# The next block's input is transposed by VectorE in place of TensorE, into a doubled place, in loops unrolled by two

## The reference

```python
xn = _layernorm(x, axis=-1)
x = x + _L0_attn_ref(xn, Wq, Wk, Wv, Wog, Wig, big, Wfg, bfg, gamma, Wout) + _L0_ffn_ref(xn, w_gate, w_up, w_down)

# attention: q, k, v, o_preact = xn @ W.T; i_pre, f_pre soft-capped at 15; 8 heads, DQ 32, DV 64
def step(carry, xs):
    C, n, m = carry
    q_t, k_t, v_t, i_t, f_t = xs
    f_log = jax.nn.log_sigmoid(f_t)
    m_new = jnp.maximum(f_log + m, i_t)
    F = jnp.exp(f_log + m - m_new)
    I = jnp.exp(i_t - m_new)
    C_new = F[..., None, None] * C + (I[..., None] * k_t)[..., :, None] * v_t[..., None, :]
    n_new = F[..., None] * n + I[..., None] * k_t
    ...
    h = h_num / denom[..., None]
...
h_norm = _multihead_norm(h, gamma).reshape(B, S, -1)
y = (jax.nn.sigmoid(o_preact) * h_norm) @ Wout.T

# ffn, 2048 hidden: gated = silu(x @ w_gate.T) * (x @ w_up.T); gated @ w_down.T
```

## Time and profile before

| | |
|---|---|
| median of 3 runs | 3141.33 us (3140.83 to 3141.61) |
| the profiled execution | 3142.2 us, with a span of 3140.4 us from the first to the last instruction |
| granted TensorE clock, mean | 0.995 |
| busy: PE, PE weight loads, DVE, ACT, POOL | 98%, 71%, 61%, 36%, 24% |

### The profile page before, as it was taken

The page is one execution under the profiler, slowest core; times in us unless marked ns, Lnnn a source line. Parts: engine busy times, 40 slices in busy tenths (PEclk is TensorE's granted clock), DMA queues, the critical chain, the costliest instruction groups (busy, mean ns, idle before and its releaser), DMA issues.

```text
span 3140.4 us, 61802 instructions
## 1 busy us (share of the span) xinstructions
PE 3077.6 (98%) x22450; PEld 2238.5 (71%) x22450; DVE 1914.3 (61%) x4380; ACT 1120.7 (36%) x2150; POOL 751.4 (24%) x1120
## 2 busy tenths in 40 slices
PE   3999999999999999999999999999999999999999
PEld 2677777777777777777777777777777777777776
DVE  8666656656556666556566566565566665665665
ACT  5333333333323333333333333333233333333332
POOL 4222222222222221222222222222222212222222
PEclk8999999999999999999999999999999999999999
DMA  5000000000000000000000000000000000000000
GB/s 222 8 14 13 13 7 7 13 13 13 13 0 13 13 13 13 7 7 13 13 13 13 7 7 13 13 13 13 0 13 13 13 13 7 7 13 13 13 13 7
DMA packets 20333, 51.08 MB, mean 16 GB/s; under 512 B 1506, under 2 KB 1634, under 8 KB 18274
## 3 DMA queue, kind: packets, MB, share of 16 engines
q1 hardware_dynamic: 20322, 50.95, 4.4%
HBM read 34.16 MB, written 16.78 MB: 16 GB/s over the span
## 4 chain that ended last, share of the span: by engine, by line
PE 97%; DVE 2%; issue 0%; DMA 0%; ACT 0%; SPq 0%; DVEq 0%; ACTq 0%
PE work L1082 21%; PE work L1084 21%; PE work L1083 21%; PE acc L1083 7%; PE acc L1084 7%; PE acc L1082 7%; PE o_bank L1189 3%; PE o_bank L1249 2%; PE work L1255 2%; PE s_bank L1236 1%; PE work L1267 1%; PE work L1261 1%; PE e_bank L1230 1%; PE work L1166 1%; DVE amax L732 1%; PE work L1221 1%
## 5 line engine op out<-in xcount | busy, mean ns | idle before, releaser
L1082 PE MATMUL work<-xt,weights 128*128 128x256 f16 x4608 | 1257.0, 273 | 0.1
L1084 PE MATMUL work<-xt,weights 128*128 128x256 f16 x4608 | 1256.8, 273 | 0.0
L1083 PE MATMUL work<-xt,weights 128*128 128x256 f16 x4608 | 1256.8, 273 | 0.0
L543 POOL TENSOR_TENSOR arena<-arena 128x256 f16<-128x256 f32 x512 | 348.6, 681 | 1715.4 <-ACT arena L670 1715.4
L955 DVE SCALAR_TENSOR_TENSOR arena<-arena,work 128x256 f32<-128x256 f32 x512 | 215.2, 420 | 537.9 <-ACT arena L666 534.8
L1082 PEld LDWEIGHTS work<-xt,weights 128*128 128x128 f16 x4608 | 478.8, 104 | 69.8 <-DVE arena L958 0.2
L1083 PEld LDWEIGHTS work<-xt,weights 128*128 128x128 f16 x4608 | 451.2, 98 | 69.9
L1084 PEld LDWEIGHTS work<-xt,weights 128*128 128x128 f16 x4608 | 451.1, 98 | 52.5
L666 ACT ACTIVATE arena<-work,unscale 128x256 f32<-128x256 f32 x512 | 241.2, 471 | 587.1 <-PE work L1084 586.7
L670 ACT ACTIVATE arena<-arena 128x256 f16<-128x256 f32 x512 | 213.4, 417 | 589.1 <-DVE arena L958 589.1
L1082 PE MATMUL acc<-weights,arena 128*128 128x512 f16 x1024 | 388.2, 379 | 0.0
(11 more groups left out here) (209 smaller groups left out, 4024.1 us busy)
## 6 DMA issues: line engine op xcount, KB each, us to landing
arena<-x_dram SPq DMA_DIRECT2D x33, 512.0 KB, 3.3
out_dram<-arena SPq DMA_DIRECT2D x32, 512.0 KB, 2.8
weights<-w_g_dram SPq DMA_DIRECT2D x4, 1024.0 KB, 13.4
weights<-w_u_dram SPq DMA_DIRECT2D x4, 1024.0 KB, 20.8
arena<-w_d_dram SPq DMA_DIRECT2D x4, 1024.0 KB, 26.3
arena<-w_qk_dram SPq DMA_DIRECT2D x1, 1024.0 KB, 6.5
arena<-w_v_dram SPq DMA_DIRECT2D x1, 1024.0 KB, 8.5
weights<-w_o_dram SPq DMA_DIRECT2D x1, 1024.0 KB, 15.9
```

Of the source, the lines that this page charges most:

```text
L543: g.tensor_tensor(hh[:, j % HB, 1, :], tt[:, j % 2, :], hh[:, j % HB, 0, :], ALU.subtract).then_inc(h_ready, 1)
L1082: t.matmul(dst, w[0], a[0], start=first, stop=False, skip_group_check=True)
L1083: t.matmul(dst, w[0], a[1], start=False, stop=False, skip_group_check=True)
L1084: return t.matmul(dst, w[1], a[0], start=False, stop=last, skip_group_check=True)
```

## The change

The order of the steps on all engines changes. mean_var goes behind tile 3, xn0 behind tile 4, xn1 behind tile 6. ScalarE now writes the normalized chunks into the places of `qs` and `kf`. A new step "turn c q" on VectorE transposes 32 tokens of chunk c: four VectorE transposes (of 32x32 blocks), each from the 32 partitions of quarter q to one of the four groups of 32 partitions, 32x128 fp32 elements each, into `xnt` in SBUF. Behind tile 5 stand turn00, turn01, turn02; behind tile 6 turn03; behind tile 7 turn10, turn11; behind tile 9 turn12, turn13. "xT0" (behind tile 7) and "xT1" (behind tile 11) are no longer on TensorE: they are only the high and the low half, now read from SBUF. `xt` has two places, used in turn, so every loop body is written for two blocks (`one_block` called twice in a loop of 16). xT0 and xT1 leave `USES`, which has 34 entries; att1 is put into bank 1. `gates` waits for the semaphore xt_ready. In the part ahead of the loop the places of the first input change, and GpSimd clears qq and kk after the first input was transposed.

The diff, cut to its core (left out: the names and the place of the new buffers, `xt` handed on as an argument, and the same loop of pairs on the other engines):

```diff
--- before.py
+++ after.py
@@ -54,18 +54,19 @@
 
 USES = (["gates", "q", "k", "v0", "v1", "ffn0", "ffn1", "ffn2", "ffn3", "wT", "ffn4", "wbc", "kT", "ffn5", "o0",
          "ffn6", "st0", "ffn7", "ffn8", "st1", "ffn9", "ffn10", "st2", "ffn11", "hoT0", "ffn12", "st3", "o1",
-         "ffn13", "att0", "ffn14", "ffn15", "hoT1", "xT0", "xT1", "att1"])
+         "ffn13", "att0", "ffn14", "ffn15", "hoT1", "att1"])
 NUSE = len(USES)
-assert NUSE % 3 == 0
+BANK = {name: n % 3 for n, name in enumerate(USES)}
+BANK["att1"] = 1
 
 
 def bank_no(name):
-    return USES.index(name) % 3
+    return BANK[name]
 
 
 def uses_of(b, before=NUSE):
 
-    return len(USES[b:before:3])
+    return len([name for name in USES[:before] if BANK[name] == b])
 
 
 
@@ -81,18 +82,20 @@
 AFTER[0] = ["stack0"]
 AFTER[1] = ["stack1"]
 AFTER[2] = ["stack2", "stats"]
-AFTER[3] = ["wT", "stack3"]
-AFTER[4] = ["wbc", "kT", "es0"]
-AFTER[5] = ["o0", "mean_var"]
-AFTER[6] = ["es1", "pv0", "xn0"]
+AFTER[3] = ["wT", "stack3", "mean_var"]
+AFTER[4] = ["wbc", "kT", "es0", "xn0"]
+AFTER[5] = ["o0", "turn00", "turn01", "turn02"]
+AFTER[6] = ["es1", "pv0", "turn03", "xn1"]
+AFTER[7] = ["turn10", "turn11", "xT0"]
 AFTER[8] = ["es2", "pv1", "center0"]
-AFTER[9] = ["scale0", "xn1"]
+AFTER[9] = ["scale0", "turn12", "turn13"]
 AFTER[10] = ["heads0", "es3", "pv2"]
-AFTER[11] = ["hoT0"]
+AFTER[11] = ["hoT0", "xT1"]
 AFTER[12] = ["pv3", "o1", "center1"]
 AFTER[13] = ["att0", "scale1"]
 AFTER[14] = ["heads1"]
-AFTER[15] = ["hoT1", "xT0", "xT1"]
+AFTER[15] = ["hoT1"]
+TURNS = 16
 
 
 UNIT_IN = {j + 1: int(step[-1]) for j in AFTER for step in AFTER[j] if step.startswith("pv")}
...
@@ -254,7 +257,9 @@
             stage["d", k] = in_arena((2, 3, 4, 0)[k])
         stage["out", 0] = in_arena(1)
         xin = at["xin"].rearrange("p (c d) -> p c d", c=NCH)
-        xn = at["xn"].rearrange("p (c d) -> p c d", c=NCH)
+        xn_first = at["kk"].rearrange("p (c d) -> p c d", c=NCH)
+        xn = at["qs"], at["kf"]
+        xnt = at["kp"], arena[:, starts["lf"]:starts["lf"] + D]
 
         qs = at["qs"].rearrange("p (g t) -> p g t", g=NG)
         qi = at["qi"].rearrange("p (g t) -> p g t", g=NG)
...
@@ -599,20 +610,19 @@
                     ins = s.activation(low(n, k)[:, c * D:(c + 1) * D], low_banks[c][:, :], ACT.Copy)
                 ins.then_inc(w_split_act, 1)
 
-            def x_high(i, c, src):
+            def x_high(xt, c, src):
                 s.activation(xt[:, :, 0, c * P:(c + 1) * P], src.rearrange("p (k t) -> p k t", k=KC),
                              ACT.Copy).then_inc(xt_hi, 1)
 
-            def norm_x(i, c):
-
-                act.wait_ge(factors_ready, i + 1)
-                s.activation(xn[:, c, :], xin[:, c, :], ACT.Identity, bias=shift[:, c:c + 1],
+            def norm_x(dst, c):
+                s.activation(dst, xin[:, c, :], ACT.Identity, bias=shift[:, c:c + 1],
                              scale=rstd[:, c:c + 1]).then_inc(xn_ready, 1)
 
+            act.wait_ge(factors_ready, 1)
             for c in range(NCH):
-                norm_x(0, c)
+                norm_x(xn_first[:, c, :], c)
                 act.wait_ge(first_xt, c + 1)
-                x_high(0, c, (e_bank, s_bank)[c][:, :])
+                x_high(xts[:, 0, :, :, :], c, (e_bank, s_bank)[c][:, :])
             for r, names in enumerate(GROUPS):
                 act.wait_ge(w_scaled, r + 2 if names == ["out"] else r + 1)
                 for n, k in pieces(names):
...
@@ -700,12 +710,22 @@
                             s.activation(ho[:, 0, :, :], bank(step)[:, :].rearrange("p (k t) -> p k t", k=KC),
                                          ACT.Copy).then_inc(ho_hi, 1)
                         elif step.startswith("xn"):
-                            norm_x(i + 1, k)
+
+                            if k == 0:
+                                act.wait_ge(factors_ready, i + 2)
+                                act.wait_ge(qi_ready, i + 1)
+                            else:
+                                wait_full(act, i, "kT")
+                            norm_x(xn[k], k)
                         elif step.startswith("xT"):
 
-                            wait_full(act, i, step)
-                            x_high(i + 1, k, bank(step)[:, :])
+                            act.wait_ge(xn_turned, START + (i * NCH + k + 1) * TURNS)
+                            x_high(xts[:, (n_ + 1) % 2, :, :, :], k, xnt[k])
                 own.close()
+
+            with act.Fori(0, NB // 2) as pair_no:
+                for n_ in range(2):
+                    one_block(pair_no * 2 + n_, n_)
 
         @block.vector
         def _(dve):
@@ -796,11 +816,19 @@
                 for c in range(NCH):
                     d.bn_aggr(mean_var[:, c, :], bn6[:, c, :]).then_inc(stats_ready, 1)
 
-            def x_low(i, c, src, done):
+            def x_low(i, xt, c, src):
 
                 dve.wait_ge(xt_hi, NCH * i + c + 1)
                 d.tensor_tensor(xt[:, :, 1, c * P:(c + 1) * P], src.rearrange("p (k t) -> p k t", k=KC),
-                                xt[:, :, 0, c * P:(c + 1) * P], ALU.subtract).then_inc(done, 1)
+                                xt[:, :, 0, c * P:(c + 1) * P], ALU.subtract).then_inc(xt_ready, 1)
+
+            def turn(dst, src, q, done):
+
+                tokens = slice(q * 32, (q + 1) * 32)
+                for r in range(P // 32):
+                    features = src[tokens, :].rearrange("t (k r f) -> t r k f", k=KC, f=32)[:, r, :, :]
+                    d.transpose(dst.rearrange("p (k t) -> p k t", k=KC)[r * 32:(r + 1) * 32, :, tokens],
+                                features).then_inc(done, 1)
 
             back = 1.0 / (XS * WS)
 
...
@@ -1059,8 +1087,11 @@
                             d.tensor_tensor(ho[:, 1, :, :], bank(step)[:, :].rearrange("p (k t) -> p k t", k=KC),
                                             ho[:, 0, :, :], ALU.subtract).then_inc(free_of(step), 1)
                         elif step.startswith("xT"):
-                            wait_full(dve, i, step)
-                            x_low(i + 1, k_, bank(step)[:, :], free_of(step))
+                            x_low(i + 1, xts[:, (n_ + 1) % 2, :, :, :], k_, xnt[k_])
+                        elif step.startswith("turn"):
+                            c = int(step[-2])
+                            dve.wait_ge(xn_ready, NCH * (i + 1) + c + 1)
+                            turn(xnt[c], xn[c], k_, xn_turned)
                         elif step == "att0":
                             add_mlstm(i, 0)
                 for c in range(NCH):
...
@@ -1159,7 +1195,7 @@
 
 
                 wait_bank(pe, i, "gates")
-                pe.wait_ge(work_free[bank_no("xT1")], START + i * uses_of(bank_no("xT1")))
+                pe.wait_ge(xt_ready, NCH * (i + 1))
 
                 for k in range(KC):
                     for half in range(2):
...
@@ -1255,12 +1291,6 @@
                             t.matmul(bank(f"st{k}")[:, 0:GW], kt[:, c, g * P:(g + 1) * P],
                                      v[:, c, g * HG:(g + 1) * HG, :], start=True,
                                      stop=True).then_inc(work_full, 1)
-                        elif step.startswith("xT"):
-                            pe.wait_ge(xn_ready, NCH * (i + 1) + k + 1)
-                            for n in range(KC):
-                                tr = t.transpose(bank(step)[:, n * P:(n + 1) * P], xn[:, k, n * P:(n + 1) * P],
-                                                 ident[:, :])
-                            tr.then_inc(work_full, 1)
                         elif step.startswith("hoT"):
                             pe.wait_ge(ho_ready, START + i * NCH + k + 1)
                             for n in range(KC):
@@ -1273,6 +1303,10 @@
                 down(NJ - 1)
                 wait_bank(pe, i, "att1")
                 project(1)
+
+            with pe.Fori(0, NB // 2) as pair_no:
+                for n_ in range(2):
+                    one_block(pair_no * 2 + n_, n_)
 
 
 # ---- launch ----
```

More of the change, by code:

```diff
@@ L215, in mlstm_mlp_kernel @@
         sc = {n: i for i, n in enumerate(WNAMES)}
-        xt = sb("xt", [P, KC, 2, BLOCK], F16)
+        xts = sb("xt", [P, 2, KC, 2, BLOCK], F16)
         we_r = sb("we_r", [GR, BLOCK], F32R)
@@ L239, in mlstm_mlp_kernel @@
             at[name] = arena[:, starts[name]:starts[name] + n]
-        assert 5 * SLOT + GCOLS <= starts["xn"]
+        assert 5 * SLOT + GCOLS <= starts["qq"]
         def in_arena(n):
@@ L331, in mlstm_mlp_kernel @@
         xt_hi = sem("xt_hi")
+        xn_turned = sem("xn_turned")
         xt_ready = sem("xt_ready")
@@ L514, in _ @@
             link(g.memset(uhl, 0.0))
+            pool.wait_ge(first_xt, NCH)
             for name in ("qq", "kk", "wr", "tg", "state"):
@@ L526, in _, with one_block @@
             pool.wait_ge(ready_set, 1)
-            with pool.Fori(0, NB) as i:
+            def one_block(i):
                 own = Count(pool_own, 8)
@@ L567, in _ @@
                 own.close()
```

(28 more changed lines are left out.)

6 lines of the change are left out of this document (3 added, 3 removed).

## The result

| | median | profiled execution's span |
|---|---|---|
| before | 3141.47 us (4 runs, 3140.83 to 3141.82) | 3140.4 us |
| changed | 3163.77 us (4 runs, 3163.26 to 3167.19) | 3162.5 us |

The ratio is 1.0073, 95% interval 1.0061 to 1.0085: 22.3 us slower. I had forecast 3123.2 us, 18 us faster. The time is inside the wide range and on the wrong side; none of the three rivals describes most of it.

A forecast was written before the change was run, and what follows sets the result against it. TensorE, 98% busy and almost never waiting, was taken as the bound. -27.8 us for removed transposes, +5.9 at q and +3.8 at ffn12 gave -18.1, from 3141.33 to 3123.2 us; range 3117 to 3190 us.

The forecast's parts named there:

- three rivals: Gain eaten up at ffn12 (0.27); transpose columns cost double (0.27); TensorE's freed time unused, down(15) awaiting GpSimd (0.04).
- Loops: Jumps back of the engines' loops: two blocks a round halve them, with no gain and no loss seen.
- the stall at ffn12: TensorE's ffn12 waits for L1005 to free bank 1: 0.12 us a block, 3.8 us in all.
- p: Time from one VectorE transpose to the next within a turn: 0.31 us, bounds 0.20 and 0.45.
- the lever of 20 transposes: No idle time on VectorE between tiles 6 and 10, so tile 10 starts 20 times later than p grows.
- the term of 4.35 us: VectorE, tile 10's start to L1005's end: between 3.8 and 4.5 us, taken as 4.35.
- Rival 1: At ffn12: each transpose takes 32 more columns, p 0.345, stall 0.82 us, gain eaten up, 3146 us; chance 0.27.
- This case's own range: Whole kernel, forecast case: 3117 us (no ffn12 stall, 0.14 at q) to 3131 us (0.28 and 0.24).
- the transposes' 0.87 us a block: TensorE's two xT steps go: 0.87 us, 32 times, 27.8 us saved.
- q's wait: TensorE's q waits for VectorE's L895 to free att1's bank: 0.19 us at 31 boundaries, 5.9 us.
- The place that decides: turn12 and turn13 on VectorE before tile 10: it starts 2.6 us late, delaying L1005 and so ffn12.
- down(15): TensorE step moved up to 1031.55 us, needing GpSimd's low half of tile 15: 0.18 us left, no cost taken.

The follow-up runs named there:

- e1: Kernel before with every engine's loop written for two blocks and nothing else: 3164.93 us, ratio 1.0074.
- e4: Changed kernel without the unrolling: one place of xt, both halves of the next input behind tile 15, read from SBUF: 3122.93 us, ratio 0.9941.
- e11: Changed kernel, still unrolled, with only xT0 moved from behind tile 7 to behind tile 11: 3145.41 us, ratio 1.0013.
- e5: e4 with turn12 and turn13 moved from behind tile 9 to behind tile 12: 3117.96 us, ratio 0.9925.
- e8: Changed kernel, still unrolled, with turn12 and turn13 behind tile 12 and xT1 behind tile 14: 3143.45 us, ratio 1.0006.
- e7: e4 with turn12 and turn13 behind tile 12 and att1 in bank 2: 3113.49 us, ratio 0.9911.
- e6: e4 with att1 in bank 2 in place of bank 1: 3118.48 us, ratio 0.9928.
- e10b: e4 with all four transposes of a turn writing partitions 0 to 31, a VectorE wait before each turn, halves taken before transposition (output differs): 3117.86 us.
- e2: Kernel before with TensorE's loop alone written for two blocks: 3147.18 us, ratio 1.0021.
- e12: Kernel before with VectorE's loop alone written for two blocks: 3163.85 us, ratio 1.0072.
- e9: Kernel before with every loop written for four blocks, 7 jumps back: 3152.71 us, ratio 1.0035.

## Why the prediction was wrong, point by point

**Two steps failed,** and either alone takes away the forecast gain.

The first is "Loops": "no gain to be had, and I see none to lose". I had judged the jump by the kernel before, where it is free, and took that for a property of the jump. It was a property of the loop's body: with two blocks in it, instructions are brought in anew at each jump. Put at nothing, this measures 25.8 us in the changed kernel (gates late by 1.72 us, 15 times). The unrolling alone costs 23.7 us in the kernel before (e1), there by VectorE's late start. Between e4 and e11 lie 22.5 us, between e5 and e8 25.5 us.

The second is the stall at ffn12: 0.12 us and 3.8 us in all by the forecast, 0.63 to 0.73 us and 21.8 us by the trace. Rather more than half of the error is p. Forecast 0.31 us, measured 0.33, and the lever of 20 transposes was right: 20 x 0.02 = 0.4 us; tile 10 starts 1012.66 - 1008.64 = 4.02 us ahead of where ffn12 would, before it was 1102.81 - 1095.88 = 6.93, so it is 2.91 us later, forecast 2.59. The rest is the term of 4.35 us from tile 10's start to L1005's end. It measures 4.59 to 4.69, for L1025 waits for GpSimd's mask even when L1081 is over. Rival 1 (p 0.345, stall 0.82) was nearer to the stall than my own value, by its number and not by its reason: 32 columns more would have made one transpose 0.28 + 0.035 = 0.315 us long; it is 0.302.

That e4 measures 3122.9 us against the 3123.2 forecast is partly luck. e4 has no low half between tiles 7 and 8, which took about as much off ffn12 as the two errors had put on it. The change's own order of steps without the unrolling was not run; with 0.14 us at q and 0.73 at ffn12 in each block it would, as an estimate, be 3141.3 - 27.8 + 4.3 + 23.4 = 3141 us, no gain at all. ("This case's own range" was also added up wrongly by a microsecond: its terms give 3118 to 3130 us, not 3117 to 3131.)

**Right:** the transposes' 0.87 us a block (e7: 95.41 - 94.53 = 0.88). q's wait, 0.19 forecast, 0.14 measured (e6), though in the changed kernel only where no jump is ahead of it: 2 us and not 5.9. The place that decides, tile 10 and then L1005 in front of ffn12 (e5, e10b, e11). Tile 4, xn0 and the twelve transposes behind tile 5 cost nothing. down(15) cost nothing.

**The sum again**, by the trace of the changed kernel: -27.8 for the transposes, +2.2 at q, +21.8 at ffn12 (16 x 0.63 + 16 x 0.73), +25.8 at the jumps: +22.0, and the spans differ by 22.1 us. By medians: -18.5 for e4 with its waits (3141.4 to 3122.9), +22.5 to e11 for the unrolling, +18.4 for xT0's place (to 3163.8): +22.4 us.

**Why the gap at gates differs.** It is 1.4 to 2.0 us long in all 15 rounds of the changed kernel, e8 and e11, but in e1 the waits name it 7 times (4.4 us) and in e2 3 times (3.2 us). The single packets tell the two kinds apart. The 16 KB that TensorE's jump needs start about 1.0 us after it, in some rounds 1.6. At all 45 jumps of the first three runs another packet of 16 KB started 0.3 to 1.0 us ahead of them, and they took 1.7 to 2.7 us. In e1 that is so at 4 jumps and in e2 at 3, and those have the gaps of about 1 us and more (packets of 1.5 to 2.1 us); where the packet comes alone it took 0.9 to 1.4 us, and gates was at most 0.4 us late. So the long gap goes with a second transfer just ahead of the one that is needed. That the other packet is the next piece in a straight line, sent for shortly before the loop's end, is my reading; no run moves the loop's end to test it. The changed kernel's q14 also carries 175 packets against e1's 100: five more in each round, which by their times (the first 0.9 to 1.2 us after each of ScalarE's jumps) are ScalarE's. It goes through 282 instructions a round there and 274 in e1, where it has none.

**Open:** what decides whether a body stays, since 473 instructions of VectorE and 282 of ScalarE didn't and 274 did.

## What to carry to other kernels

Before unrolling a hardware loop, look at the instruction packets of the page: if there are next to none, the body stays with the engines and the jump is free, and a longer body may change both at once. The engine to look at is not only the bottleneck's: in the kernel before, VectorE's late start alone cost 22.6 us and TensorE's alone 5.9, because VectorE's chain behind the jump has no slack to take it up. The two don't add up (e1 costs 23.7 us): where TensorE itself is late, VectorE's lateness is covered.

Where a chain of small operations is laid ahead of a release, the error in one operation's time counts as often as there are operations without idle time between them; move them to where the engine idles, and it counts no more (e5). And follow the chain up to the release: here a wait for a third engine's mask made it 0.24 to 0.34 us longer than forecast.

## What the runs showed of the hardware that was not expected

- One block's instructions (239 on VectorE, 1470 on TensorE) are run over and over, through 31 jumps back, with no instruction packet. With two blocks' (473), each jump back costs VectorE 2.3 us of "issue" (e12: 34.7 us in 15), and the kernel 22.6 us in all.
- Instructions that are brought in ahead in a straight line cost nothing (e9: about e1's packets, half its price, and 95.4 us for a block with no jump at either end).
- A 16 KB instruction packet of TensorE's jump took 1.7 to 2.7 us where another had started 0.3 to 1.0 us ahead of it (changed kernel, e8, e11), and 0.9 to 1.4 us where it came alone (e1, e2).
- A VectorE transpose of 32x128 fp32 takes 302 ns and 0.33 us from start to start if the next one writes other partitions; 257 ns (median) and 0.22 us if it writes the same (e10b).
